# A two-layer attention and feed-forward network: expert tiles and layer 1's rotation put into one stage

## The chip, the cores and the metric

One core of one Trainium2 chip runs the kernel. The metric is the device time of one execution in microseconds (us). The core has TensorE (PE; its weight loads are PEld), VectorE (DVE), ScalarE (ACT), GpSimd (POOL), SyncE (SP, here only a queue of DMAs) and 16 DMA engines. Names such as `a_ov` or `q_ps` are on-chip tensors; TensorE writes to PSUM, which GpSimd doesn't reach.

## The reference

A sequence of 2048 tokens of 128 numbers goes through two layers. Each layer is `x + attention(xn) * silu(ffn(xn))`, with `xn` the layer norm of x. All is float32.

```python
# layer 1 (H = 16 heads of 64, E = 8 experts, F = 512)
q, k, v = split(xn @ qkv_w.T)                       # 16 heads each
q, k = rope(q), rope(k)      # t1*c - t2*s, t1*s + t2*c over the two halves of a head
attn = softmax(q @ k.T * 0.125 - p * log1p(a * |i - j|))
s = (attn @ v) @ out_w.T
probs = softmax(xn @ Wr + br); idx = argmax(probs)  # one expert a token
h = relu((layernorm(xn) * g + b) @ W1[idx] + b1[idx])
y = (h @ W2[idx] + b2[idx]) * max(probs)
x = x + s * silu(y)
```

Layer 0 has attention without rotation and bias, and a feed-forward with ternary weights and gelu.

## The kernel before

The program is a row of stages. Each is a block in which every engine has an instruction list written out by hand, ordered against the others by semaphores; a stage ends when all engines and its DMAs are through. For layer 1 they are:

`layernorm_stage` (L84), which leaves `xnT`, the transposed activations.

`route_stage` (L995). TensorE multiplies `xnT` by the router weights (L1057). A long chain of small VectorE steps takes the maximum, the one-hot choice and running counts; TensorE adds the counts over the partitions (`tot` and `pos`, L1061 to L1063); from these comes for each token its place in a list sorted by expert, padded to 23 tiles (`TL`) of 128 tokens of one expert each. Then VectorE normalizes and scales each of the 16 token tiles (L1126 to L1131) and GpSimd scatters it to the DRAM tensor `sorted_in` (L1050). SP loads all experts' weights meanwhile, the first matrices into `w1` and the second into a part of `va`.

`expert_tiles_stage` (L1151). TensorE spreads the biases, reads the owner of each of the 23 tiles from `tiles` into registers (`value_load`), and then works a tile at a time: transposes of four tiles at once (L1211), four upward products (L1222) with the weights that GpSimd has picked from `w1` (L1256), relus shared by ScalarE (L1277) and VectorE (L1295), a bias product (L1231) and four downward products (L1236). VectorE copies the results out (L1288), SP stores them to `sorted_out` (L1193). While tile i is up, tile i-1 goes down.

`qkv_stage(nc, k, 1, w1, rope=table)` (L367). First 16 value tiles: two 128x512 products each (L536), half copied by ScalarE (L490), half by VectorE (L447), to `va`. Meanwhile GpSimd gathers each token's result from `sorted_out` into `gate` (L512) and copies layer 1's output weights into `wo` (L515). Then 32 rotation jobs, one for each of 8 pairs of heads, q or k, and half of the sequence: TensorE makes the product with the weights and with a copy of them whose halves are exchanged and signed (`wsw`, L443, L550), 1024 columns of each; VectorE multiplies the first by the cosines and the second by the sines (L464, L465); GpSimd adds the two (L518); ScalarE rounds the sum to float16, the high part (L502); VectorE subtracts this from the sum, the low part (L455), two jobs late. SP stores both (L406, L407). `t1` and `t2` have three buffers, the float16 parts two. At the end ScalarE applies silu to `gate` (L506).

`attention_stage(nc, k, 1, bias=True)` (L565). SP loads q, k and a table of biases (L629 to L637). GpSimd clears tensors (L922 to L925). VectorE takes maxima over 16 pieces (L840), ScalarE turns them into a row (L772, L777), then for each of 512 steps: scores (L688), bias added by VectorE (L878), exponent by ScalarE (L784), values (L699), sums by GpSimd (L943).

Of the kernel before, what the change touches and what calls it, by code (L numbers as in the profile page):

```python
# [564 lines left out]
def attention_stage(nc, k, layer, bias=False):  # L565

    with ExitStack() as ctx:
# [25 lines left out]
        added = m.sem(g + "added") if bias else None  # L593
# [172 lines left out]
        def _(act):  # L766
# [152 lines left out]
        def _(pool):  # L919
# [62 lines left out]
def experts_stage(nc, k, t, fetched):  # L982

    with ExitStack() as outer:
# [3 lines left out]
        w1 = mo.sb("ex_w1", [D, NE, FF])  # L988
        scattered, weights_loaded = mo.sem("ex_scattered"), mo.sem("ex_weights_loaded")
        w2 = flat(k.va[:, :, :])[:, 0:FT * NE * D].rearrange("p (j e d) -> p j e d", j=FT, e=NE)  # L990
        route_stage(nc, k, t, tiles, hot, w1, w2, scattered, weights_loaded)
        expert_tiles_stage(nc, k, t, tiles, hot, w1, w2, scattered, weights_loaded, fetched)


def route_stage(nc, k, t, tiles, hot, w1, w2, scattered, weights_loaded):  # L995

    with ExitStack() as ctx:
# [19 lines left out]
        tot = m.ps("rt_tot", [P, NE])  # L1017
        loaded, affine_loaded, made, counted, chain = (m.sem("rt_loaded"), m.sem("rt_affine"), m.sem("rt_made"),
# [8 lines left out]
        def _(sp):  # L1027
# [4 lines left out]
            sp.dma_start(w1[:, :, :], t["L1_ffn_W1"].rearrange("e m f -> m e f")).then_inc(weights_loaded, 16)  # L1032
# [5 lines left out]
        def _(pool):  # L1038
# [7 lines left out]
            nc.gpsimd.memset(ends[:, :, 0:NE], 0.0).then_inc(counted, 1)  # L1046
            pool.wait_ge(placed, 1)
# [6 lines left out]
        def _(pe):  # L1054
            pe.wait_ge(loaded, 32)
            for q in range(NT):
                last = nc.tensor.matmul(ps[:, q, :], k.xnT[:, q * P:(q + 1) * P], wr[:, :], start=True, stop=True)  # L1057
            last.then_inc(made, 1)
            pe.wait_ge(counted, 6)
# [4 lines left out]
                             start=False, stop=True).then_inc(ranked, 1)  # L1064

# [78 lines left out]
        def _(act):  # L1144
            act.wait_ge(var_done, 1)
            nc.scalar.activation(std[:, :], std[:, :], ACT.Sqrt).then_inc(std_done, 1)
            act.wait_ge(shifted, 1)
            nc.scalar.activation(e[:, :, :], e[:, :, :], ACT.Exp).then_inc(exped, 1)


def expert_tiles_stage(nc, k, t, tiles, hot, w1, w2, scattered, weights_loaded, fetched):  # L1151

    with ExitStack() as ctx:
        m = Memory(nc, ctx)
        b1, b2 = m.sb("ep_b1", [NE, FF]), m.sb("ep_b2", [NE, D])
        b1t = m.sb("ep_b1t", [P, FT, TL])
        room = flat(k.va[:, :, :])[:, FT * NE * D:]
        xs = room[:, 0:TL * D].rearrange("p (i d) -> p i d", d=D)
        xsT = room[:, TL * D:2 * TL * D].rearrange("p (i q) -> p i q", q=P)
        ys = room[:, 2 * TL * D:3 * TL * D].rearrange("p (i d) -> p i d", d=D)  # L1160
        hT = room[:, 3 * TL * D:3 * TL * D + 2 * FF].rearrange("p (b j q) -> p b j q", b=2, j=FT)
        w1i = m.sb("ep_w1i", [P, 2, FF])
        tp = m.ps("ep_tp", [P, 2, 4, P])
        up = m.ps("ep_up", [P, 2, 2, 512])
        dn = m.ps("ep_dn", [P, 2, 4, D])
        bt = flat(dn[:, 1, :, :])[:, 0:FT * TL].rearrange("p (j i) -> p j i", j=FT)
        loaded, xs_loaded, turned, xs_copied = (m.sem("ep_loaded"), m.sem("ep_xs_loaded"), m.sem("ep_turned"),
                                                m.sem("ep_xs_copied"))
        spread, b1_copied, up_done = m.sem("ep_spread"), m.sem("ep_b1_copied"), m.sem("ep_up_done")
        w1_picked = m.sem("ep_w1_picked")  # L1170
        relu_act, relu_dve, dn_done, y_copied = (m.sem("ep_relu_act"), m.sem("ep_relu_dve"), m.sem("ep_dn_done"),
                                                 m.sem("ep_y_copied"))
        block = ctx.enter_context(nc.Block())
        NG = (TL + 3) // 4

        def members(g):
            return range(4 * g, min(4 * g + 4, TL))

        @block.sync
        def _(sp):  # L1180
            sp.dma_start(b1[:, :], t["L1_ffn_b1"]).then_inc(loaded, 16)
            sp.dma_start(b2[:, :], t["L1_ffn_b2"]).then_inc(loaded, 16)
            sp.wait_ge(scattered, 16 * NT)
            for g in range(NG):
                a, b = 4 * g, members(g)[-1] + 1
                sp.dma_start(xs[:, a:b, :], k.sorted_in[a * P:b * P, :].rearrange("(i p) d -> p i d", p=P))\
                  .then_inc(xs_loaded, 16)
                if g % 2 == 1 or g == NG - 1:
                    sp.wait_ge(xs_loaded, 16 * (g + 1))
            for g in range(NG):  # L1190
                a, b = 4 * g, members(g)[-1] + 1
                sp.wait_ge(y_copied, g + 1)
                sp.dma_start(k.sorted_out[a * P:b * P, :].rearrange("(i p) d -> p i d", p=P), ys[:, a:b, :])\  # L1193
                  .then_inc(fetched, 16)
            sp.wait_ge(fetched, 16 * NG)

        @block.tensor
        def _(pe):
            pe.wait_ge(loaded, 32)
            for j in range(FT):  # L1200
                last = nc.tensor.matmul(bt[:, j, :], b1[:, j * P:(j + 1) * P], hot[:, :], start=True, stop=True)
            last.then_inc(spread, 1)
            owners = [pe.value_load(tiles[0:1, i:i + 1], min_val=0, max_val=NE - 1) for i in range(TL)]

            def turn(g):
                if g % 2 == 0:
                    pe.wait_ge(xs_loaded, 16 * min(g + 2, NG))
                if g >= 2:
                    pe.wait_ge(xs_copied, g - 1)
                for i in members(g):  # L1210
                    last = nc.tensor.transpose(tp[:, g % 2, i % 4, :], xs[:, i, :], k.ident[:, :])  # L1211
                last.then_inc(turned, 1)

            def upward(i):
                if i % 4 == 0:
                    pe.wait_ge(xs_copied, i // 4 + 1)
                pe.wait_ge(w1_picked, i + 1)
                if i >= 2:
                    pe.wait_ge(relu_act, i - 1)
                    pe.wait_ge(relu_dve, i - 1)  # L1220
                for j in range(FT):
                    last = nc.tensor.matmul(up[:, i % 2, j // 2, (j % 2) * P:(j % 2 + 1) * P], w1i[:, i % 2, j * P:(j + 1) * P], xsT[:, i, :],  # L1222
# [3 lines left out]
            def downward(i):  # L1226
                g = i // 4
                o = dn[:, g % 2, i % 4, :]
                if i % 4 == 0 and g >= 2:
                    pe.wait_ge(y_copied, g - 1)  # L1230
                nc.tensor.matmul(o, hot[:, i:i + 1].broadcast_to([NE, P]), b2[:, :], start=True, stop=False)  # L1231
                pe.wait_ge(relu_act, i + 1)
                pe.wait_ge(relu_dve, i + 1)
# [5 lines left out]
            turn(0)  # L1239
            pe.wait_ge(weights_loaded, 16 * (1 + FT))  # L1240
            for i in range(TL):
                if i % 4 == 0 and i // 4 + 1 < NG:
                    turn(i // 4 + 1)
                upward(i)
                if i >= 1:
                    downward(i - 1)
            downward(TL - 1)

        @block.gpsimd
        def _(pool):  # L1250
            pool.wait_ge(weights_loaded, 16 * (1 + FT))
            for i in range(TL):
                owner = pool.value_load(tiles[0:1, i:i + 1], min_val=0, max_val=NE - 1)
                if i >= 2:
                    pool.wait_ge(up_done, i - 1)
                nc.gpsimd.tensor_copy(w1i[:, i % 2, :], w1[:, bass.ds(owner, 1), :].rearrange("p a f -> p (a f)"))                  .then_inc(w1_picked, 1)  # L1256

        @block.scalar
        def _(act):
            act.wait_ge(spread, 1)  # L1260
# [3 lines left out]
            def copy_x(g):  # L1264
                act.wait_ge(turned, g + 1)
                n = len(members(g))
                nc.scalar.activation(xsT[:, 4 * g:4 * g + n, :], tp[:, g % 2, 0:n, :], ACT.Copy).then_inc(xs_copied, 1)

            copy_x(0)
            for i in range(TL):  # L1270
                if i % 4 == 0 and i // 4 + 1 < NG:
                    copy_x(i // 4 + 1)
                act.wait_ge(up_done, i + 1)
                if i >= 2:
                    act.wait_ge(dn_done, i - 1)
                for j in range(2):
                    last = nc.scalar.activation(hT[:, i % 2, j, :], up[:, i % 2, 0, j * P:(j + 1) * P], ACT.Relu,  # L1277
                                                bias=b1t[:, j, i:i + 1])
                last.then_inc(relu_act, 1)

        @block.vector
        def _(ve):
            ve.wait_ge(b1_copied, 1)

            def copy_y(g):
                ve.wait_ge(dn_done, members(g)[-1] + 1)
                n = len(members(g))
# [91 lines left out]
```

## Time and profile before

| what | us |
|---|---|
| median of 3 runs | 3075.92 (3074.8 to 3075.96) |
| the profiled execution | 3079.59 |
| its span | 3077.9 |
| PE, DVE, ACT, POOL busy | 2807.8, 2504.0, 1557.4, 2502.6 |
| mean granted TensorE clock | 0.964 |

The span is the time from the first to the last instruction that the profiler recorded. Busy times of the engines overlap. A granted clock of 1.00 is TensorE's full 2.4 GHz, 0.50 is 1.2 GHz. Attention takes some 85% of the span (layer 0 to 1431 us, layer 1 from 1730 us); the stages that the change touches lie between.

### The profile page before, as it was taken

To read this page: it belongs to the slowest core of one execution; us is meant where nothing else is said; L and a number is where in the kernel's file an instruction comes from. 1 tells how busy PE (TensorE), PEld (TensorE's weight loads), DVE (VectorE), ACT (ScalarE), POOL (GpSimd) and SP (SyncE) were. 2 spreads that over 40 slices of the span, in tenths; PEclk is the share of its full clock that TensorE was granted. 3 is DMA by queue.
4 is the path that set the end of the run, shared out by engine and by line. 5 is a ranking of instruction groups with operands and counts; after the bars stand their busy time and mean duration, and the time that the engine had idled before them with its cause. 6 is when DMAs were issued, how large, how long until landed. Compare 5 with 4: busy or idle time off the path is not lost. (4 is left out here: it accounts for less than half of the span.)

```text
span 3077.9 us, 46733 instructions
## 1 busy us (share of the span) xinstructions
PE 2807.8 (91%) x17656; PEld 1147.6 (37%) x17656; DVE 2504.0 (81%) x3379; ACT 1557.4 (51%) x1889; POOL 2502.6 (81%) x1205
## 2 busy tenths in 40 slices
PE   5959999999999999996499599999999999999997
PEld 3413333333333333333354133333333333333332
DVE  6568888888888888874339699999999999999995
ACT  4325555555555555552122255555555555555554
POOL 0009999999999999994339389999999999999997
PEclk9979999999999999997699699999999999999998
DMA  4250111111111111101203501111111111111100
GB/s 109 86 191 22 35 29 28 28 28 28 28 28 28 28 29 28 28 1 38 60 27 137 190 4 52 55 55 55 55 55 55 55 55 55 55 55 55 55 1 14
DMA packets 63825, 155.28 MB, mean 50 GB/s; under 512 B 18017, under 2 KB 33770, under 8 KB 61426
## 3 DMA queue, kind: packets, MB, share of 16 engines
q1 hardware_dynamic: 62578, 150.20, 17.4%
q8 instruction: 141, 2.31, 0.3%
q0 software_dynamic: 1024, 2.10, 0.2%
q14 instruction: 82, 0.67, 0.1%
HBM read 113.34 MB, written 38.93 MB: 49 GB/s over the span
## 5 line engine op out<-in xcount | busy, mean ns | idle before, releaser
L943 POOL TENSOR_TENSOR a_sums<-a_sums,room 128x1024 f32<-128x1024 f32 x512 | 1195.4, 2364 | 83.1 <-ACT room L795 42.5
L699 PE MATMUL a_ov<-room,va 128*64 128x512 f32 x4096 | 994.0, 606 | 0.0
L784 ACT ACTIVATE room<-room,sscale 128x1024 f32<-128x1024 f32 x512 | 588.3, 1149 | 539.3 <-DVE room L878 539.2
L845 DVE TENSOR_REDUCE a_mx<-a_jb 128x1 f32<-128x1024 f32 x501 | 611.9, 1221 | 129.6 <-PE a_jb L653 123.4
L943 POOL TENSOR_TENSOR a_sums<-room 128x1024 f32<-128x1024 f32 x256 | 604.3, 2361 | 116.6 <-ACT room L784 66.8
L840 DVE CUSTOM_DVE_ANT_0 a_junk<-a_jb,a_tab 128x1024 bf16<-128x1024 f32 x501 | 610.5, 1219 | 83.2 <-PE a_jb L653 74.8
L878 DVE TENSOR_TENSOR room<-a_st,a_tab 128x1024 f32<-128x1024 f32 x512 | 622.9, 1217 | 12.4 <-PE a_st L688 10.2
L795 ACT ACTIVATE room<-a_st,sscale 128x1024 f32<-128x1024 f32 x256 | 285.3, 1114 | 360.1 <-PE a_st L688 360.1
L652 PE MATMUL a_jb<-a_kh,a_qh 64*128 64x512 f16 x1002 | 384.9, 384 | 66.1 <-DVE a_mx L840 32.1
L699 PEld LDWEIGHTS a_ov<-room,va 128*64 128x64 f32 x4096 | 248.7, 136 | 409.3 <-issue 372.7
L688 PE MATMUL a_st<-a_qh,a_kh 64*128 64x512 f16 x2048 | 395.6, 383 | 3.0 <-DVE a_mx L840 2.9
L688 PE MATMUL a_st<-a_ql,a_kh 64*128 64x512 f16 x2048 | 390.8, 378 | 0.0
L688 PE MATMUL a_st<-a_qh,a_kl 64*128 64x512 f16 x2048 | 390.6, 378 | 0.0
L865 DVE SCALAR_TENSOR_TENSOR room<-a_rows,a_st 128x1024 f32<-128x1024 f16 x256 | 312.7, 1221 | 92.3 <-PE a_st L688 90.9
L653 PE MATMUL a_jb<-a_kh,a_qh 64*128 64x512 f16 x1002 | 385.1, 384 | 0.0
L788 ACT ACTIVATE room<-room,sscale 128x1024 f32<-128x1024 f32 x256 | 294.0, 1148 | 170.8 <-DVE room L865 170.8
L946 POOL TENSOR_TENSOR a_sums<-a_sums 128x1024 f32<-128x1024 f32 x128 | 302.8, 2366 | 10.1
L688 PE MATMUL a_st<-a_rows,a_lower 64*128 64x512 f16 x1536 | 292.9, 378 | 0.0
L652 PEld LDWEIGHTS a_jb<-a_kh,a_qh 64*128 64x128 f16 x1002 | 93.6, 93 | 465.8 <-DVE a_mx L845 306.3
L688 PEld LDWEIGHTS a_st<-a_qh,a_kh 64*128 64x128 f16 x2048 | 99.8, 94 | 274.0 <-issue 164.1
L950 POOL TENSOR_TENSOR a_total<-a_sums 128x512 f32<-128x512 f32 x128 | 162.5, 1270 | 10.0
L710 PE MATMUL a_xb<-ones,a_total 128*128 128x1 f32 x1024 | 136.4, 254 | 17.3 <-POOL a_total L950 17.3
(219 smaller groups left out, 2642.6 us busy)
## 6 DMA issues: line engine op xcount, KB each, us to landing
a_tab<-bias_line SPq DMA_DIRECT2D x16, 1984.0 KB, 11.0
qk_high<-q_oh SPq DMA_DIRECT2D x32, 512.0 KB, 2.6
qk_low<-q_ol SPq DMA_DIRECT2D x32, 512.0 KB, 3.6
a_qh<-qk_high SPq DMA_DIRECT2D x64, 256.0 KB, 4.5
a_kh<-qk_high SPq DMA_DIRECT2D x64, 256.0 KB, 5.1
a_ql<-qk_low SPq DMA_DIRECT2D x64, 256.0 KB, 7.5
a_kl<-qk_low SPq DMA_DIRECT2D x64, 256.0 KB, 7.8
ex_w<-in_L_ffn_W SPq DMA_DIRECT2D x1, 2048.0 KB, 10.5
```

The lines of the kernel that those rows point to most:

```text
L652: nc.tensor.matmul(o[:, 0:QC], qh[0:DH, q0:q0 + P], kh[0:DH, k0:k0 + QC], start=True, stop=True)
L653: nc.tensor.matmul(o[:, QC:2 * QC], qh[DH:P, q0:q0 + P], kh[DH:P, k0 + QC:k0 + 2 * QC], start=True, stop=True).then_inc(max_ready, 1)
L688: last = nc.tensor.matmul(st[:, step % 2, t * QC:(t + 1) * QC], w, x, start=(r == 0), stop=(r == len(rounds) - 1))
L699: last = nc.tensor.matmul(ov[t * DH:(t + 1) * DH, :], k.va[:, 2 * s + t, h * DH:(h + 1) * DH], prob[:, step % RING, t * QC:(t + 1) * QC], ...
L784: nc.scalar.activation(prob[:, r, :], prob[:, r, :], ACT.Exp, scale=k.sscale[:, layer:layer + 1])\
L788: nc.scalar.activation(prob[:, r, :], prob[:, r, :], ACT.Exp, scale=k.sscale[:, 0:1])\
L840: nc.vector.tensor_tensor_reduce(out=junk[:, i % 2, :], in0=scratch(n, j), in1=tab[:, n // NC % 2, c0:c0 + 2 * QC][:, ::-1], scale=1.0, sc ...
L845: nc.vector.reduce_max(mx[:, j // 2, j % 2:j % 2 + 1], scratch(n, j), AX.X).then_inc(max_done, 1)
L865: nc.vector.scalar_tensor_tensor(p, high, -float(MAXROW), x, ALU.mult, ALU.add).then_inc(lowered, 1)
L878: nc.vector.tensor_tensor(p[:, :, ::-1], x[:, :, ::-1], window, ALU.add).then_inc(added, 1)
L943: nc.gpsimd.tensor_tensor(a, first, prob[:, step % RING, :], ALU.add).then_inc(summed, 1)
L946: nc.gpsimd.tensor_tensor(a, a, sums[:, (n + 1) % 2, :], ALU.add).then_inc(summed, 1)
```

## The change

Three stages (route, expert tiles, q/k/v of layer 1) become two.

In the route stage TensorE also makes the first 8 value tiles, three of them ahead of the rank products `tot` and `pos`, five behind; ScalarE copies them to `va`. GpSimd regroups the q and k weights into `wo`: for each group of four heads, the first halves of the heads side by side (128 columns), then the second halves. The second experts' and first experts' weights both go to the second half of `va`, so `ex_w1` is gone. The expert biases are loaded here.

`experts_and_rotation_stage` does the rest. It has 16 rotation jobs: 4 groups of four heads, q or k, half of the sequence. A job makes the product with the first halves (`low_part`) and with the second halves (`high_part`), one PSUM buffer of 1024 columns each. VectorE multiplies each by cosines and by sines (four multiplies), GpSimd subtracts two and adds two, ScalarE makes two high parts and VectorE two low parts, one job late. Into TensorE's and ScalarE's lists two expert tiles are put in each of jobs 1 to 11 and one in job 12, behind the job's own work (`project` on TensorE, `high_halves` of the job before on ScalarE); the last 8 value tiles go into jobs 12 to 15. ScalarE does all that other engines did for the tiles: the picks, all four relus, both copies. Transposes and downward results have one PSUM buffer instead of two. TensorE and ScalarE each read the 23 owners into registers.

The gathers and silus move into the attention stage: the gathers behind GpSimd's clears, the silus behind ScalarE's first row and ahead of its first exponent.

```diff
@@ attention_stage, ScalarE and GpSimd @@
             divide_maxima(0)
             row(0)
+            if bias:
+                act.wait_ge(gathered, 16 * NT)
+                for q in range(NT):
+                    nc.scalar.activation(k.gate[:, q, :], k.gate[:, q, :], ACT.Silu, scale=k.prob[:, q:q + 1])
...
             nc.gpsimd.memset(lower[DH:DH + 1, :], -float(MAXROW)).then_inc(ones_set, 1)
+            if bias:
+                for q in range(NT):
+                    nc.gpsimd.indirect_dma_start(k.gate[:, q, :], None, k.sorted_out[:, :],
+                                                 bass.IndirectOffsetOnAxis(ap=k.spot[:, q:q + 1], axis=0))\
+                      .then_inc(gathered, 16)
@@ route_stage, GpSimd, TensorE, ScalarE @@
+            for i in range(2):
+                for r in range(2):
+                    nc.gpsimd.tensor_copy(grouped[:, i, r, :, :], halves[:, i, :, r, :])
             pool.wait_ge(placed, 1)
...
             last.then_inc(made, 1)
+            def values_of(q):
+                if q >= 2:
+                    pe.wait_ge(val_copied, q - 1)
+                for c in range(2):
+                    last = nc.tensor.matmul(val[:, q % 2, c * QC:(c + 1) * QC], k.xnT[:, q * P:(q + 1) * P],
+                                            k.w1[:, 2, c * QC:(c + 1) * QC], start=True, stop=True)
+                last.then_inc(valued, 1)
+            for q in range(3):
+                values_of(q)
             pe.wait_ge(counted, 6)
             pe.wait_ge(added, 1)
...
+            for q in range(3, NVAL):
+                values_of(q)
...
+            for q in range(NVAL):
+                act.wait_ge(valued, q + 1)
+                nc.scalar.activation(k.va[:, q, :], val[:, q % 2, :], ACT.Copy).then_inc(val_copied, 1)
@@ experts_and_rotation_stage, TensorE @@
+            def project(j):
+                g, i, half = jobs[j]
+                for r, (part, ready) in enumerate(((low_part, a_ready), (high_part, b_ready))):
+                    if j >= 1:
+                        pe.wait_ge(prod, 4 * (j - 1) + 2 * r + 2)
+                    for c in range(2):
+                        q0 = half * 1024 + c * 512
+                        last = nc.tensor.matmul(part[:, c * 512:(c + 1) * 512], wqk[:, i, r, g * P:(g + 1) * P],
+                                                k.xnT[:, q0:q0 + 512], start=True, stop=True)
+                    last.then_inc(ready, 1)
...
+            project(0)
+            owners = [pe.value_load(tiles[0:1, i:i + 1], min_val=0, max_val=NE - 1) for i in range(TL)]
             pe.wait_ge(weights_loaded, 16 * (1 + FT))
+            for j in range(NJOB):
+                if j >= 1:
+                    project(j)
+                for i in work[j]:
...
+                    if i % 4 == 0 and i // 4 + 1 < NG:
+                        turn(i // 4 + 1)
+                    upward(i)
+                    if i >= 1:
+                        downward(i - 1)
...
+                for q in late[j]:
+                    values_of(q)
@@ ScalarE @@
+            for j in range(NJOB):
+                if j >= 1:
+                    high_halves(j - 1)
+                for i in work[j]:
+                    if i == 0:
+                        copy_x(0)
+                    if i % 4 == 0 and i // 4 + 1 < NG:
+                        copy_x(i // 4 + 1)
+                    act.wait_ge(up_done, i + 1)
+                    if i >= 2:
+                        act.wait_ge(dn_done, i - 1)
+                    for f in range(FT):
+                        last = nc.scalar.activation(hT[:, i % 2, f, :], up[:, i % 2, f, :], ACT.Relu,
+                                                    bias=b1t[:, f, i:i + 1])
+                    last.then_inc(relu_done, 1)
+                    if i + 2 < TL:
+                        pick(i + 2)
+                    if i % 4 == 0 and i >= 4:
+                        copy_y(i // 4 - 1)
...
@@ VectorE and GpSimd @@
+            def low_halves(j):
+                for r, rotated in enumerate((first, second)):
+                    ve.wait_ge(high, 2 * j + r + 1)
+                    nc.vector.tensor_tensor(split[:, j % 2, 1, r, :], rotated[:, j % 2, :], split[:, j % 2, 0, r, :],
+                                            ALU.subtract).then_inc(low, 1)
+            for j, (g, i, half) in enumerate(jobs):
+                b, sl = j % 2, slice(half * 1024, (half + 1) * 1024)
+                ve.wait_ge(a_ready, j + 1)
...
+                nc.vector.tensor_tensor(first[:, b, :], low_part[:, :], cos[:, sl], ALU.mult).then_inc(prod, 1)
+                nc.vector.tensor_tensor(second[:, b, :], low_part[:, :], sin[:, sl], ALU.mult).then_inc(prod, 1)
+                ve.wait_ge(b_ready, j + 1)
...
+                nc.vector.tensor_tensor(product[:, 0, :], high_part[:, :], sin[:, sl], ALU.mult).then_inc(prod, 1)
...
+                nc.vector.tensor_tensor(product[:, 1, :], high_part[:, :], cos[:, sl], ALU.mult).then_inc(prod, 1)
+                if j >= 1:
...
+                    low_halves(j - 1)
...
+                pool.wait_ge(prod, 4 * j + 3)
+                nc.gpsimd.tensor_tensor(first[:, b, :], first[:, b, :], product[:, 0, :], ALU.subtract).then_inc(rot, 1)
+                pool.wait_ge(prod, 4 * j + 4)
+                nc.gpsimd.tensor_tensor(second[:, b, :], second[:, b, :], product[:, 1, :], ALU.add).then_inc(rot, 1)
+            nc.gpsimd.tensor_copy(flat(k.wo[:, :, :]), flat(k.wo1[:, :, :]))
```

## Rows read from the trace of the kernel before

**Rows 1.** Windows by stage: length, busy time of each engine (instructions), granted clock, DMA, GB/s.
```profile
1449.00:1491.50 42.50, 8.62 (x38) 8.26 (x38) 26.21 (x114) 1.81 (x3) 16.93 (x22) 0.50 0.45 127
1491.50:1571.50 80.00, 62.38 (x445) 56.19 (x445) 18.04 (x52) 18.12 (x53) 14.17 (x23) 0.86 0.14 39
1571.50:1730.40 158.90, 143.06 (x320) 59.37 (x320) 126.22 (x114) 49.43 (x65) 120.38 (x49) 0.95 0.29 113
```

**Rows 2.** Groups, q/k/v stage: busy us, mean ns, idle before and its releaser.
```profile
L502 ACT ACTIVATE q_oh<-q_t 128x1024 f16<-128x1024 f32 x32 | 33.8, 1057 | 88.3 <-POOL q_t L518 88.3
L515 POOL COPY wo<-wo 128x2048 f32<-128x2048 f32 x1 | 1.9, 1907 | 0.0
```

**Rows 3.** Timeline, q/k/v stage: start us, us, instruction, idle before in brackets.
```profile
1577.49 0.60 ACT L490 ACTIVATE va<-q_ps 128x512 f32<-128x512 f32 x1 [1.12 <-PE q_ps L536]
...
1616.48 1.23 DVE L464 TENSOR_TENSOR q_t<-q_ps,rope 128x1024 f32<-128x1024 f32 x1
1617.62 1.22 DVE L465 TENSOR_TENSOR q_t<-q_ps,rope 128x1024 f32<-128x1024 f32 x1
1618.75 1.22 DVE L455 TENSOR_TENSOR q_ol<-q_t,q_oh 128x1024 f16<-128x1024 f32 x1
1620.07 1.23 DVE L464 TENSOR_TENSOR q_t<-q_ps,rope 128x1024 f32<-128x1024 f32 x1
```

**Rows 4.** Timeline of GpSimd, the rotation's first jobs.
```profile
1608.47 2.35 POOL L518 TENSOR_TENSOR q_t<-q_t 128x1024 f32<-128x1024 f32 x1 [13.42 <-DVE q_t L465]
...
1618.92 3.27 POOL L518 TENSOR_TENSOR q_t<-q_t 128x1024 f32<-128x1024 f32 x1 [0.32 <-DVE q_t L465]
```

**Rows 5.** Line L455 (min/median/max ns), then the timeline at the rotation's end.
```profile
L455 DVE TENSOR_TENSOR q_ol<-q_t,q_oh x32: 1215/1215/3361, 1615.2 to 1724.3; 128x1024 f16<-128x1024 f32 x32
...
1719.68 4.49 DVE L455 TENSOR_TENSOR q_ol<-q_t,q_oh 128x1024 f16<-128x1024 f32 x2
1719.84 3.25 POOL L518 TENSOR_TENSOR q_t<-q_t 128x1024 f32<-128x1024 f32 x1 [0.34 <-DVE q_t L465]
...
1724.34 1.23 DVE L455 TENSOR_TENSOR q_ol<-q_t,q_oh 128x1024 f16<-128x1024 f32 x1 [0.17 <-ACT q_oh L502]
```

**Rows 6.** Timeline of the expert tiles.
```profile
1515.49 1.06 PE L1222 MATMUL ep_up<-va,ep_w1i 128*128 128x128 f32 x8
...
1516.59 0.63 ACT L1277 ACTIVATE va<-ep_up,ep_b1t 128x128 f32<-128x128 f32 x2 [1.77 <-PE ep_up L1222]
...
1517.89 1.06 PE L1222 MATMUL ep_up<-va,ep_w1i 128*128 128x128 f32 x8
...
1520.92 0.60 ACT L1267 ACTIVATE va<-ep_tp 128x512 f32<-128x512 f32 x1 [1.31 <-PE ep_tp L1211]
```

**Rows 7.** Timeline of the tile stage's start; last a window, columns as in rows 1.
```profile
1493.35 1.90 PE L1201 MATMUL ep_dn<-ex_hot,ep_b 8*128 8x23 f32 x8 [28.52 <-DMA ep_b<-in_L_ffn_b]
1508.59 1.96 PE L1211 MATMUL ep_tp<-ident,va 128*128 128x128 f32 x8 [13.34 <-issue]
...
1514.00:1515.00 1.00, 1.00 (x8) 0.80 (x7) 0.61 (x2) 0.62 (x2) 0.62 (x1) 1.00 0.00 0
```

**Rows 8.** The route stage: the group of the scatters, then its timeline.
```profile
L1050 POOL DMA_INDIRECT sorted_in<-acc,spot x16 | 15.9, 992 | 23.4 <-DVE acc L1131 19.7 <-issue 3.6
...
1452.03 7.00 PE L1057 MATMUL rt_ps<-rt_w,room 128*128 128x8 f32 x32 [3.91 <-DMA rt_b<-in_L_ffn_br]
1463.21 0.56 PE L1061 MATMUL rt_tot<-rt_before,ones 128*128 128x8 f32 x2 [4.18 <-DVE rt_before L1107]
```

**Rows 9.** Timeline of the attention stage's start.
```profile
1733.30 0.20 POOL L925 MEMSET a_lower<- 1x128 f16 x1
...
1754.63 1.28 ACT L784 ACT_TABLE_LOAD   x1
...
1766.05 1.23 DVE L878 TENSOR_TENSOR room<-a_st,a_tab 128x1024 f32<-128x1024 f32 x1 [1.95 <-PE a_st L688]
```

More of the change, by code:

```diff
@@ L1169, in expert_tiles_stage @@
[L1169 to L1172, printed above, removed]
+        b1t = m.sb("er_b1t", [P, FT, TL])
+        first, second, product = (m.sb("er_first", [P, 2, 1024]), m.sb("er_second", [P, 2, 1024]),
+                                  m.sb("er_product", [P, 2, 1024]))
@@ L1173, in expert_tiles_stage, with xs @@
         block = ctx.enter_context(nc.Block())
         NG = (TL + 3) // 4
+        jobs = [(g, i, half) for g in range(4) for i in range(2) for half in range(2)]
+        NJOB = len(jobs)
+        work = [[i for i in range(TL) if 1 + i // 2 == j] for j in range(NJOB)]
+        late = [[q for q in range(NVAL, NT) if NJOB - (NT - q + 1) // 2 == j] for j in range(NJOB)]
         def members(g):
             return range(4 * g, min(4 * g + 4, TL))
+        def xs(a, b):
+            return k.acc[:, a:b, :] if b <= NT else xs_more[:, a - NT:b - NT, :]
@@ L1179, in _, with xsT @@
+        def xsT(a, b):
+            return xsT_first[:, a:b, :] if b <= NT else xsT_more[:, a - NT:b - NT, :]
         @block.sync
         def _(sp):
[L1181 to L1189, printed above, removed]
@@ new lines, in store_qk @@
+            def store_qk(j):
+                g, i, half = jobs[j]
+                sp.wait_ge(low, 2 * j + 2)
+                for n, store in enumerate((k.qk_high, k.qk_low)):
+                    rows = store[i].rearrange("a p s -> (a p) s").rearrange("(g h r d) s -> g r h d s", g=4, h=4, r=2)
+                    for r in range(2):
+                        sp.dma_start(rows[g, r, :, :, half * 1024:(half + 1) * 1024], split[:, j % 2, n, r, :])\
+                          .then_inc(stored[j % 2], 16)
@@ L1197, in _ @@
+            for b in range(2):
+                sp.wait_ge(stored[b], 64 * (NJOB // 2))
+            sp.wait_ge(y_stored, 16 * NG)
         @block.tensor
         def _(pe):
[L1199 to L1203, printed above, removed]
+            def project(j):
+                g, i, half = jobs[j]
+                for r, (part, ready) in enumerate(((low_part, a_ready), (high_part, b_ready))):
[6 more added lines that the diff above has]
+                    last.then_inc(ready, 1)
@@ L1237, in downward @@
                 last.then_inc(dn_done, 1)
-            turn(0)
-            pe.wait_ge(weights_loaded, 16 * (1 + FT))
[L1241 to L1256, printed above, removed]
+            pe.wait_ge(biases_loaded, 32)
@@ L1258, in _, with pick, copy_values @@
         @block.scalar
         def _(act):
+            owners = [act.value_load(tiles[0:1, i:i + 1], min_val=0, max_val=NE - 1) for i in range(TL)]
+            act.wait_ge(weights_loaded, 16 * (1 + FT))
+            def pick(i):
+                nc.scalar.activation(w1i[:, i % 2, :], w1[:, bass.ds(owners[i], 1), :].rearrange("p a f -> p (a f)"),
+                                     ACT.Copy).then_inc(picked, 1)
+            def copy_values(q):
+                for c in range(2):
+                    act.wait_ge(valued, 2 * (q - NVAL) + c + 1)
+                    nc.scalar.activation(k.va[:, q, c * QC:(c + 1) * QC], flat(up[:, c, :, :]), ACT.Copy)\
+                      .then_inc(val_copied, 1)
@@ L1266, in copy_x @@
                 n = len(members(g))
[L1267 to L1279, printed above, removed]
+                nc.scalar.activation(xsT(4 * g, 4 * g + n), tp[:, 0:n, :], ACT.Copy).then_inc(xs_copied, 1)
```

186 lines of the change are left out of this document (122 added, 64 removed).

## The prediction, made before the kernel was changed

> **What bounds the kernel now.** I read the windows by stage first [rows 1]. The change touches the 281 us from 1449.0 to 1730.4 (route, expert tiles, layer 1's q/k/v) and the first 36 us of the attention after it. In the route stage every engine is mostly idle; in the tiles TensorE is busy 62 of 80 us and VectorE 18; in the q/k/v stage VectorE is busy 126 of 159 us. So the expert tiles are TensorE's, the rotation is VectorE's, and one could lie beside the other.
>
> ScalarE's high half is 1.06 us [rows 2]. One value tile is two 128x512 float32 products, and while TensorE sets the pace a copy of 0.60 us comes after 1.12 us of waiting for it [rows 3]: 1.72 us a tile, so the four products of a rotation job are 3.43 us.
>
> The timeline of VectorE [rows 3] shows such a job: two multiplies that start 1.14 us apart, then the subtract that makes the low half, next job 1.32 us after it starts: 3.59 us a job, 115 us for 32. GpSimd's add [rows 4] took 2.35 us when no subtract was near and 3.27 us when it was issued at 1618.92, 0.17 us behind the subtract at 1618.75. Read as a lock: the subtract holds something for about 1.09 us, the add waits 0.92 us and then takes its 2.35. The end of the stage shows the other order [rows 5]: an add issued at 1719.84 waits for the subtract of 1719.68, ends at 1723.09 (again 0.9 + 2.35), and the next subtract, issued at about 1720.8, ends only at 1724.17: the two subtracts are 4.49 us instead of about 2.4. A multiply, which reads one operand from PSUM, shows no such thing: it is 1.22 us beside adds throughout [rows 3, 4].
>
> The Trainium skill says the same in "SBUF — State Buffer", section "Who interferes with whom": a VectorE instruction with two SBUF inputs and a GpSimd instruction that reads SBUF exclude each other for a whole instruction, and "issue order, not op shape, decides who blocks". The trace agrees in both orders (3.27 against 2.35 us for the add, 4.49 us for two subtracts).
>
> In the tile stage [rows 6] a tile is 2.40 us of TensorE (1515.49 to 1517.89), two relus are 0.63 us on ScalarE, a four-tile copy 0.60. At the stage's start [rows 7] TensorE ends its bias products at 1495.25 and does nothing that the profile names ("issue") until 1508.59: those are the 23 value_loads of the owners, 13.3 us, 0.58 each. It then works at 0.50 of the clock and is at 1.00 from 1514: 5.4 us at the lower level (1.2 GHz) after an idle stretch.
>
> **The change part by part.**
>
> Route stage. GpSimd's four regrouping copies fall into the 19.7 us in which it waits for the first scaled tile [rows 8]; the whole 128x2048 copy is 1.91 us [rows 2], so four quarters are 2 to 4 us: nothing. If they reached past that wait the stage would end later by the excess. The scatters then take 15.9 + 3.6 = 19.5 us and end the stage, so whatever delays VectorE's rank chain delays all. Here something does: three value tiles stand on TensorE between the router products (end 1459.0) and the rank products (start 1463.2) [rows 8]. They are 5.2 us at full clock (rank products start at 1464.2, which then run at twice the speed: +0.4) and 10.3 us at half (+6.2). I take 5.4 us at the lower level and the rest at the upper, as in rows 7: 7.9 us, +3.8, less 0.8 for faster rank products: **+3.0 us**. The other five value tiles and ScalarE's eight copies (about 1.1 each) lie under the scatters. The new stage thus starts at 1494.5 instead of 1491.5.
>
> Start of the new stage (times from its start). Bias products to 2.0 [rows 7]; project(0), cold, low part at 5.5, high part at 8.1; then the same 23 value_loads, which now stand between project(0) and project(1): 13.3 us, to 21.4. project(1) is cold again, its low part is there at 24.8: VectorE, done with job 0 at about 10.3, starts **job 1 at 24.9**. ScalarE has 23 value_loads of its own (no row; 0 to 1 us each from TensorE's 0.58; I take 0.58, done at 13.4, hidden by TensorE's; at 1 us job 1's tiles come about 1 us later).
>
> A job in the new stage is half as many (16) and twice as large: four products (3.43 us, as before), four multiplies, two subtracts, two adds, two high halves. The multiplications by the other half no longer need their own products, so TensorE's rotation work falls from 110 to 55 us; VectorE's count stays 96. In plain VectorE time a job would be 2 x 3.59 = 7.2 us. But the order has changed. With S the start of a job: multiplies at S, +1.14, +2.28, +3.42; the first add needs the third multiply and starts at +3.57; the subtracts of the job before are issued from +4.55, while the add is running. By rows 5 the first subtract gets through at +5.92, ends about +7.0; the second add, waiting by then, goes ahead of the second subtract (as at 1720.8) to +9.33; that subtract ends at +10.4; the next job starts at **+10.6**. Both adds back to back give the same end: 3.57 + 2 x 2.35 + 2 x 1.09 = 10.45. Before, the subtract was issued 0.17 us ahead of its add and VectorE never waited. Bounds: 7.2 (no exclusion on VectorE's side) and 10.9 (full 1.22 us for each subtract).
>
> Do the tiles fit beneath 10.6 us? TensorE has 3.43 + 2 x 2.40 = 8.2 us a job, and 8.7 in every second one (four transposes, 0.45). ScalarE does the high halves first, the second at +9.4 to +10.5, then relus (1.2), picks (0.6), copies (0.6 each); in every second job the downward product waits for relu, pick and the copy of y: about 3.3 us after the second high half, so to S+4.7 of the following job with its own 1.4 us. project's low part is then ready at +6.4, needed at +10.6. So the 23 tiles cost nothing beside VectorE, and the 80 us stage goes; without the exclusion that chain is what is late next (rivals). ScalarE sums to 2.1 + 2 x 1.8 + 1.2 = 6.9 us a job. The last eight value tiles (3.43 us a job in four jobs) and their copies fit too. The stores are as many bytes; four issues a job instead of two for each pair of halves.
>
> End: job 15 starts at 24.9 + 14 x 10.6 = 173.3. Its second add ends at +9.3, job 14's subtract at +10.4, the weights' copy (1.9 us, GpSimd) goes next to +12.3, the last two subtracts end at +14.5. Before, the last subtract ended at 1725.57 and the next stage began at 1730.4, 4.8 us later, for stores and the barrier [rows 1, 5]; two more issues make it about 5.9: **193.7 us** for the stage.
>
> Attention of layer 1. Sixteen gathers (1.22 us each, 19.5) follow the memsets that end 3.1 us into the stage [rows 9]: last issue at 22.6, landed about 25.5 (estimate). ScalarE is free at 24.2 (1754.63), then a table load of 1.28, 16 silus (no row; 0.3 each as a half of a two-relu group, rows 6) 4.8, another load: with the landing at 25.5 about 32.9. The first exponent needs VectorE's sum that ends at 1767.27, 36.9: hidden with 4 us to spare. If that cover fails, every us past it is paid. The gathers share the DMA engines with the table that opens the stage; a MB beside 3.4 MB costs 0 to 4 us, I take **+2**. The silus that left the old stage ended together with its last stores, so their going gives under 1 us, counted in the end above.
>
> **Sum.** Old: 1491.5 to 1730.4. New end: 1494.5 + 193.7 = 1688.2, that is 42.2 us earlier; less 2: 40.2. The profiled execution took 3079.6 (span 3077.9 and 1.7 around it), 3.7 above the median of the runs, 3075.9; the difference is subtracted from the median: **3036 us**.
>
> **Rivals.**
>
> A. VectorE gets its second subtract in ahead of the waiting add, or is not held at all: for it speaks that the median old subtract took 1.215 us [rows 5], most with an add behind it; against it that the longest, 3.361 us, is the one which met an add that was first. Then TensorE and ScalarE set the pace: with the second add ending near +10.2 beside the subtracts, the downward product of every second job waits for high half, copy, relu, pick and copy, a 10.0 us job, the others 8.2; with the late value jobs the stage is 170 us: **3012**. With the adds also at 2.35 us and jobs at 7.2, about 2995.
>
> B. TensorE drops to the lower clock in the 2 to 3 us that it waits in each job and is slow to return. Each warm-up of 5.4 us costs 2.7, so a job's 8.2 to 8.7 become 10.9 to 11.4; with up to 1.3 us of waiting for ScalarE 12.5: 14 x 1.9 = 27 us more, **3062**. For it: rows 7; against: a busier TensorE waits less and so stays up.
>
> "TensorE: Matmul & The Clock Gate", section "HAM oscillation — how this bites in real kernels" of the Trainium skill describes short bursts that each start at the low clock after a wait; rows 7 show one such start, no row here a repeated one.
>
> C. The other side: TensorE stays at 1.2 GHz through the tile jobs, so that it is the bound. A job is 16.4 us, 17.4 with transposes; 11.5 such jobs cost (16.9 - 10.6) x 11.5 = 72 us: **3108**, slower. It decides from a mean tile job of 10.6 + 40.2 / 11.5 = 14.1 us. Against it: the dense tile stage rose to 1.00 within 5.4 us.
>
> D. The change doesn't overlap what it says at the seams: ranks at +6.2, ScalarE's loads slow, gathers past the first exponent by 8 us: **3050**.
>
> **How the numbers follow.** Forecast 0.55, A 0.22, B 0.09, D 0.10, C 0.04. The range from 3008 to 3058 holds the forecast, most of A and D and some of B. A measurement of this kernel tells 0.2% (6 us) from no change: faster 0.94, same 0.02, slower 0.04 (C).
>
> **What would show it.** In the changed trace: adds and subtracts of the new stage with subtracts of 2.4 to 3.4 us, VectorE's jobs 10.6 us apart while TensorE and ScalarE wait; 13 us of "issue" on TensorE after project(0); rank products 3 us later; the first exponent still released by VectorE's sum. Jobs under 9.5 us say A; a granted clock under 0.9 in the tile jobs says B or C.

## The result, and the profile after

The changed kernel takes **3056.64 us** (median of 4 runs, 3054.31 to 3060.03) beside 3075.94 for the kernel before on the same chip: ratio 0.9937, interval 0.992 to 0.9954. It is 19.3 us faster; 40 were forecast. The profiled execution took 3054.31 us, span 3052.5.

Windows of the changed kernel, columns as in rows 1: the route stage, the new stage, and a stretch near its end.
```profile
1444.60:1488.70 44.10, 23.40 (x70) 14.06 (x70) 26.17 (x114) 9.77 (x11) 19.08 (x26) 0.69 0.45 123
1488.70:1703.30 214.60, 148.77 (x605) 92.40 (x605) 161.26 (x96) 83.50 (x176) 92.11 (x33) 0.83 0.27 93
1674.00:1700.00 26.00, 1.48 (x4) 0.38 (x2) 6.34 (x4) 3.20 (x4) 5.73 (x2) 0.61 0.26 102
```
Against [rows 1] the route stage is 1.6 us longer (42.5 before), and one stage of 214.6 us replaces 80.0 + 158.9 = 238.9: 24.3 gained where the forecast had 45.2. In the last of the three windows the compute engines do little, and the DMA engines move 102 GB/s at a share of 0.26, about what four busy engines of sixteen give (0.25). The DMA records of the trace say the same: in these 26 us four packets of 2 KB, 84 ns each, are under way at once for 21.2 us and five for 4.6. In the kernel before, between 1640 and 1680, no packet is under way for 23.1 us and sixteen or seventeen for 12.2. (The changed part began 4.4 us earlier in this profiled execution than in the one before; layer 0, which is unchanged, was that much shorter.)

The start of the new stage, timeline of TensorE, then of ScalarE (start us, us, instruction, idle before).
```profile
1494.20 2.42 PE L1279 MATMUL er_high_part<-room,wo 128*128 128x512 f32 x4
1504.36 3.75 PE L1279 MATMUL er_low_part<-room,wo 128*128 128x512 f32 x4 [7.74 <-issue]
...
1501.30 1.15 ACT L1356 ACTIVATE w<-va 128x512 f32 x2 [29.05 <-issue]
```
The 23 value_loads leave TensorE idle for 7.7 us, not the 13.3 of [rows 7]: they ran, it seems, on its sequencer while the products already queued still executed. ScalarE's end at 12.6 us into the stage.

The first undisturbed job: VectorE, then GpSimd.
```profile
1508.15 1.22 DVE L1426 TENSOR_TENSOR er_first<-er_low_part,rope 128x1024 f32<-128x1024 f32 x1 [9.09 <-PE er_low_part L1279]
1509.29 1.21 DVE L1427 TENSOR_TENSOR er_second<-er_low_part,rope 128x1024 f32<-128x1024 f32 x1
1510.42 1.21 DVE L1431 TENSOR_TENSOR er_product<-er_high_part,rope 128x1024 f32<-128x1024 f32 x1
1511.56 1.21 DVE L1434 TENSOR_TENSOR er_product<-er_high_part,rope 128x1024 f32<-128x1024 f32 x1
1512.69 2.47 DVE L1418 TENSOR_TENSOR er_split<-er_first,er_split 128x1024 f16<-128x1024 f32 x1
1515.08 3.37 DVE L1418 TENSOR_TENSOR er_split<-er_second,er_split 128x1024 f16<-128x1024 f32 x1
1518.55 1.23 DVE L1426 TENSOR_TENSOR er_first<-er_low_part,rope 128x1024 f32<-128x1024 f32 x1
...
1511.72 2.36 POOL L1447 TENSOR_TENSOR er_first<-er_first,er_product 128x1024 f32<-128x1024 f32 x1 [9.05 <-DVE er_product L1431]
1514.03 3.34 POOL L1449 TENSOR_TENSOR er_second<-er_second,er_product 128x1024 f32<-128x1024 f32 x1
```
This is the exclusion of [rows 3], [rows 4] and [rows 5], in the order that was worked out: the add at 1511.72 holds the first subtract (2.47 us instead of 1.22), the second add goes ahead of the second subtract (3.37). The next job starts 10.40 us after this one.

Then comes what was not forecast: the chain from a store to VectorE. Timeline of ScalarE, TensorE and VectorE.
```profile
1532.48 1.06 ACT L1386 ACTIVATE er_split<-er_first 128x1024 f16<-128x1024 f32 x1 [8.54 <-DMA qk_low<-er_split]
...
1537.06 0.79 PE L1308 MATMUL er_dn<-ex_b,ex_hot 8*128 8x128 f32 x2 [6.15 <-ACT acc L1379]
...
1539.65 3.58 PE L1279 MATMUL er_low_part<-room,wo 128*128 128x512 f32 x4
...
1543.27 1.22 DVE L1426 TENSOR_TENSOR er_first<-er_low_part,rope 128x1024 f32<-128x1024 f32 x1 [4.03 <-PE er_low_part L1279]
```
Read it downwards. ScalarE wants to write the high half of a job into the buffer of two jobs before, whose stores haven't landed, and waits 8.5 us. Its copy `acc` (the expert's y), queued behind, is late; TensorE's downward product waits 6.2 us for it; the next rotation product, behind that, comes 4.0 us too late for VectorE. The view of waits of the new stage (engine, line, releaser: us in total, times, longest), ScalarE's and then the DMA queue's own:
```profile
ACT er_split L1386 <- DMA qk_low<-er_split: 79.5, 14, 8.5
...
SPq L1268 <- DMA qk_low<-er_split: 11.3, 1, 11.3
```
The profile page's DMA issues (KB each, median us to landing):
```profile
sorted_out<-acc SPq DMA_DIRECT2D x4, 256.0 KB, 12.2
```
A y tile of 256 KB takes 12.2 us to land; the kernel before needed 2.3 for the same transfer. And the end of the stage, VectorE then the DMA queue:
```profile
1684.64 1.22 DVE L1418 TENSOR_TENSOR er_split<-er_second,er_split 128x1024 f16<-128x1024 f32 x1
...
1687.03 4.54 SPq L1251 DMA_DIRECT2D qk_low<-er_split  x2
1703.30 0.51 SPq L629 DMA_DIRECT2D a_qh<-qk_high  x1
```
From the last subtract's end (1685.86) to the next stage are 17.4 us; 5.9 were forecast.

The arithmetic of the stores fits this: 64 of 256 KB are 16.8 MB, at 102 GB/s 164 us; a job's four are 10.3 us of transfer in a job of 10.4 us, and the y tiles' 1.5 MB queue in between.

### The profile page after: what moved, and what is told of

The parts are those of the page before. It is cut to its first block and busy times, and to the rows that moved or that the text cites. A ratio compares the mean times of both kernels' runs of the same rounds, so it can differ in the third digit from the quotient of the medians.

```text
span 3052.5 us, 46385 instructions
## 1 busy us (share of the span) xinstructions
PE 2762.6 (91%) x17528; PEld 1130.9 (37%) x17528; DVE 2520.1 (83%) x3309; ACT 1586.8 (52%) x1972; POOL 2476.2 (81%) x1186
## 3 DMA queue, kind: packets, MB, share of 16 engines
q0 software_dynamic: 1024, 2.10, 0.2%
```

## The experiments

Theory N (narrow stores): a store of the new stage names its target rows as 4 heads x 32 dimensions x 1024 columns, and the transfer is spread over as many DMA engines as that slowest dimension, 4, lets it. This is a rule of the Trainium skill, "DMA: Bandwidth & Descriptors", section "Why a DMA increments its semaphore by 16 and not by 1": the engines used are the largest number up to 16 that divides the slowest dimension of both patterns, and for one kind of queue they are always the lowest-numbered ones. The four packets at a time agree with the number; which engines they were, no row here shows. Rivals: the order of the rows in memory, SyncE's issues, or VectorE's long job itself.

**The stores' slowest dimension 32 instead of 4.** The columns of a group are put in the order dimension, head; SBUF rows follow, the rotation's frequencies are loaded in the same order (one transfer instead of four, in an early stage), and the rows written in DRAM are the same.
```
-grouped = flat(k.wo[:, :, :]).rearrange("p (i r h d) -> p i r h d", i=2, r=2, h=H)
+grouped = flat(k.wo[:, :, :]).rearrange("p (i r g d h) -> p i r g h d", i=2, r=2, g=4, h=4)
-rows = ...rearrange("(g h r d) s -> g r h d s", g=4, h=4, r=2)
+rows = ...rearrange("(g h r d) s -> g r d h s", g=4, h=4, r=2)
```


> The changed kernel with one thing else: within a group of four heads the rows are ordered by dimension first and head second (weights' columns and the angle table's partitions to match), so that the slowest dimension of each q/k store is 32 long instead of 4. Same bytes, same instructions. Theory (the stores ran on a part of the DMA engines: 102 GB/s at a DMA share of 0.26, so ScalarE waits for free buffers and the stage's end waits for the last stores): DMA share in bursts well over 0.26, no ScalarE wait for qk_low in the jobs, all jobs 10.4 us apart, stage end about 14 + 15 us earlier: 3056 - 29 = 3027 us. Rival 1 (the store path is limited by the 2 KB rows or by HBM writes, not by how it is spread): same time, 3056, still about 100 GB/s. Rival 2 (the stalls are ScalarE's order: tiles and high halves in one list): stalls stay, only the tail gains, 3041.

Measured: **3025.91 us** (3024.57 to 3028.75; ratio to before 0.9836, 0.982 to 0.9853), 30.7 below the changed kernel. Its VectorE, two jobs in the middle, and the landing of its y tiles:
```profile
1523.26 1.23 DVE L1426 TENSOR_TENSOR er_first<-er_low_part,rope 128x1024 f32<-128x1024 f32 x1
...
1533.66 1.23 DVE L1426 TENSOR_TENSOR er_first<-er_low_part,rope 128x1024 f32<-128x1024 f32 x1
```
```profile
sorted_out<-acc SPq DMA_DIRECT2D x4, 256.0 KB, 2.9
```
Jobs are 10.40 us apart without a gap, y tiles land in 2.9 us, ScalarE waits for no store, and the stage takes 184.1 us instead of 214.6. Between 1640 and 1660 no packet is under way for 14.3 us and sixteen to eighteen for 4.7: the stores come in bursts over all the engines. With the stores mended the kernel is 10 us faster than the forecast.

**VectorE's order.** The subtracts of the job before are put between the multiplies, each ahead of the add that it would meet: low part times cosines, high part times sines, first subtract, low part times sines, high part times cosines, second subtract. The waits of TensorE and GpSimd follow. Stores stay narrow.
```
-low*cos, low*sin, high*sin, high*cos, subtract, subtract
+low*cos, high*sin, subtract, low*sin, high*cos, subtract
```


> The changed kernel with VectorE's order in a job changed: low x cos, high x sin, first subtract, low x sin, high x cos, second subtract; GpSimd's adds are released accordingly. Stores as in the changed kernel. Theory of the exclusion (a subtract that finds an add running waits for its end): subtracts 1.22 us again, adds 2.35 plus at most 1.1; but the stores' 1.05 MB a job at 102 GB/s take 10.3 us, so jobs stay near 10 us apart and ScalarE's waits for stores grow: 3040 to 3056. Rival (subtracts are slow for another reason, such as their float16 output or length): they stay at 2.4 to 3.4 us. Rival to the store theory (stores do not bind): jobs 7.2 to 9 us apart, 3020 or less.

Measured: 3052.21 us (3048.11 to 3056.81; ratio 0.9925, 0.9908 to 0.9941), 4.4 below the changed kernel, whose runs overlap with these (from 3054.31). Its waits:
```profile
ACT er_split L1386 <- DMA qk_low<-er_split: 72.8, 14, 7.0
```
VectorE is quicker where no store holds it (jobs 1 to 3 start 9.2 and 8.2 us apart) and then has to wait (15.2 us to job 4): the stores are the bound of the changed kernel's stage.

**Both edits together.** The diff is the two above.

> Both edits: wide stores and the new VectorE order. If both theories hold they add up: jobs are then set by TensorE and ScalarE, 8.2 and 9.6 us alternately in the tile jobs, about 7.3 in the last ones, stage end about 56 us earlier than in the changed kernel: 3001 us. If only the stores matter 3027; if only the order 3040 to 3056.

Measured: **2999.69 us** (ratio 0.9755, 0.9739 to 0.9772). Timeline of VectorE and, last, GpSimd:
```profile
1560.17 1.23 DVE L1425 TENSOR_TENSOR er_first<-er_low_part,rope 128x1024 f32<-128x1024 f32 x1 [0.75 <-PE er_low_part L1279]
...
1563.03 1.22 DVE L1417 TENSOR_TENSOR er_split<-er_first,er_split 128x1024 f16<-128x1024 f32 x1
...
1566.43 1.22 DVE L1417 TENSOR_TENSOR er_split<-er_second,er_split 128x1024 f16<-128x1024 f32 x1
1568.83 1.22 DVE L1425 TENSOR_TENSOR er_first<-er_low_part,rope 128x1024 f32<-128x1024 f32 x1 [1.19 <-PE er_low_part L1279]
...
1563.19 3.27 POOL L1449 TENSOR_TENSOR er_first<-er_first,er_product 128x1024 f32<-128x1024 f32 x1 [1.56 <-DVE er_product L1429]
```
A subtract issued 0.16 us ahead of its add takes 1.22 us and the add 3.27, the order of [rows 4]; it is the order of issue that decides who waits, as the Trainium skill has it ("SBUF — State Buffer", section "Who interferes with whom"), and the run agrees. Now TensorE sets the pace, busy for all of the 16.88 us from 1551.95 to 1568.83: jobs of 8.66 and 8.22 us in turn, the 8.7 and 8.2 us that the prediction gave as TensorE's work. The 9.6 us expected of every second job did not appear; 10.9 us from job 12 to job 13 did, so that the sum of 3001 was met in part by luck. The same edit is worth 26.2 us beside wide stores and 4.4 beside narrow ones.

**Value_loads behind project(1)**, on top of both.
```
 project(0)
+project(1)
 owners = [pe.value_load(...) for i in range(TL)]
...
-    if j >= 1: project(j)
+    if j >= 2: project(j)
```


> As with both edits, and TensorE's 23 value_loads of the owners come after the products of job 1 instead of before. VectorE's wait of 9 us ahead of job 1 goes, but the tiles start as late as before and job 2's products stand behind the first two tiles: 0 to 2 us faster than with both edits, 3000. Rival (the whole 9 us is gained, since VectorE sets the pace): 2992.

Measured: 3005.37 us (ratio 0.9775, 0.9758 to 0.9791), 5.7 slower: a miss. TensorE, then VectorE:
```profile
1499.06 1.88 PE L1279 MATMUL er_high_part<-room,wo 128*128 128x512 f32 x4
1512.86 1.09 PE L1289 MATMUL er_tp<-ident,acc 128*128 128x128 f32 x4 [11.92 <-issue]
...
1522.53 1.23 DVE L1426 TENSOR_TENSOR er_first<-er_low_part,rope 128x1024 f32<-128x1024 f32 x1 [15.80 <-PE er_low_part L1279]
```
Job 1 starts early and job 2 late. The instructions of project(1) wait until VectorE has emptied project(0)'s products, and TensorE's sequencer with them. So only the last products (1.9 us) are queued when the loads begin, and 11.9 us are idle instead of 7.7; transposes, tile products and project(2) come after them.

**Two heads a store, and one head a store**, both on the changed kernel with its rows where they were; the counts waited for follow.
```
-sp.dma_start(rows[g, r, :, :, ...], split[:, ...])
+for h in range(0, 4, W):   # W = 2, or W = 1
+    sp.dma_start(rows[g, r, h:h + W, :, ...], split[32 * h:32 * (h + W), ...])
```


> The changed kernel with each store of four heads cut into two stores of two heads (8 issues a job instead of 4, the same rows, bytes and addresses, the semaphore's counts doubled). Theory: a store runs on as many DMA engines as the slowest dimension of its pattern lets it, the heads. With two heads it is two engines, always the same two: 51 GB/s and a share of 0.13 where four heads gave 102 GB/s and 0.26. The 16.8 MB of the stage then take 329 us instead of 164, the ScalarE and VectorE wait for the stores in every second job, and the kernel takes 3057 + 145 to 165 us: 3200 to 3225, slower than before the change. Rival (what limits the stores is the bytes, the bank behind them or the issue of SyncE, 0.6 us each and 4.8 us a job of 10.4): no longer than 3057, within 5 us.

Measured: 3207.34 us (2 runs, 3207.13 and 3207.55; ratio 1.043, 1.0409 to 1.0451). Window near the end of the stage, then the waits of the stage:
```profile
1840.00:1850.00 10.00, 0.00 (x0) 0.00 (x0) 0.00 (x0) 0.00 (x0) 0.00 (x0) 0.50 0.13 51
```
```profile
ACT er_split L1387 <- DMA qk_low<-er_split: 210.3, 14, 19.1
```
Half the slowest dimension, half the rate, 150.7 us more. In that window two packets are under way at once for 9.0 of the 10 us.

> The changed kernel with each store cut into four, one head each, so that the slowest dimension is the 32 rows of a head: 16 issues a job, 9.7 us of SyncE a job of 10.4, nothing else changed. Theory (the engines of a store are set by its slowest dimension): the stores run on 16 engines, the share in a stretch of the stage alternates between bursts and nothing, no wait for qk_low of over 1 us on ScalarE; jobs 10.4 us apart as in the run with the dimensions in the other order (3025.9), and a tail longer by 12 issues of 0.6 us: 3033 (3028 to 3040). Rival 1 (it was the order of the rows in memory or in the weights that cost): 3057. Rival 2 (SyncE's issues become the bound, as the y stores and their waits come on top of 9.7 us): jobs over 10.4 us apart, 3040 to 3055, with the SyncE busy throughout.

Measured: 3033.58 us (3032.38 to 3034.22; ratio 0.9865, 0.9848 to 0.9881). Window in mid-stage, then VectorE and the DMA queue in it:
```profile
1600.00:1620.00 20.00, 17.83 (x88) 12.52 (x87) 19.79 (x13) 10.18 (x24) 10.50 (x5) 0.92 0.46 114
```
```profile
1613.94 1.22 DVE L1427 TENSOR_TENSOR er_first<-er_low_part,rope 128x1024 f32<-128x1024 f32 x1
...
1624.32 1.23 DVE L1427 TENSOR_TENSOR er_first<-er_low_part,rope 128x1024 f32<-128x1024 f32 x1
...
1613.86 3.60 SPq L1252 DMA_DIRECT2D qk_high<-er_split  x8
1617.50 3.72 SPq L1252 DMA_DIRECT2D qk_low<-er_split  x8
```
Four times the issues (7.3 us of SyncE a job, where 9.7 were expected) and the same row order, and the jobs are back at 10.38 to 10.40 us. So it is neither the order of the rows, nor the bytes, nor the issues, but the slowest dimension: 2, 4 and 32 (in two ways) give 3207, 3057 and 3026 to 3034. The expectation's "no wait of over 1 us on ScalarE" was wrong: it waits 58.1 us in 14 pieces, 5.9 at the longest, since the last of a job's stores is issued 7 us after the first; VectorE's job is long enough to cover it.

**The value_loads in the route stage**, on top of both mends: the owners are worked out after the fourth scaled tile, and TensorE and ScalarE load them behind their value tiles, under the scatters.
```
     if q == 3:             # VectorE, after the scaled tile 3
+        ...                # reached, owner, then tiles; tiled += 1
 for q in range(3, NVAL): values_of(q)     # TensorE; ScalarE likewise
+pe.wait_ge(tiled, 1)
+k.pe_owners = [pe.value_load(...) for i in range(TL)]
```

> On top of both mends (dimension ahead of head in the stores; the VectorE's products in the order low times cos, high times sin, low times sin, high times cos), which took 2999.7 us: the tiles' owners are worked out after the fourth scaled tile of the route stage instead of at its end, and TensorE and ScalarE load them into registers there, under the scatters. Theory: the loads are 12.7 to 13.3 us of TensorE where nothing is queued in front, 7.7 beside the queued products of project(0); with them gone VectorE's job 1 starts 7.5 to 9 us earlier after the stage's start, ScalarE has its registers at once: 2991 (2989 to 2994). The five operations that come earlier on VectorE (some 1.5 us) delay the first scatters by as much only if VectorE leads them. Rival (the stage's start is held by another thing, xs tiles' loads and their landing, or ScalarE's first copies): under 3 us of gain, 2997 to 3001.

Measured: **2992.75 us** (2990.8 to 2993.51; ratio 0.973, 0.9714 to 0.9747), 6.9 less than with both mends. Timeline of TensorE in the new stage:
```profile
1501.09 1.19 PE L1284 MATMUL er_low_part<-room,wo 128*128 128x512 f32 x1 [2.54 <-DVE er_second L1439]
```
Job 1's products wait 2.5 us for VectorE, and no longer for loads. Job 1 starts 14.0 us after the stage's first product instead of 19.1: 5.1 us earlier, not the 7.5 to 9 expected, since VectorE has to empty job 0's products first. The time was met, the gain at the start was over-sized.

**All value tiles behind the rank products**, on top of that.
```
-for q in range(3): values_of(q)           # ahead of the rank products
-for q in range(3, NVAL): values_of(q)     # behind them
+for q in range(NVAL): values_of(q)
```

> As the one before, and the rank products of the route stage no longer have three value tiles of layer 1 ahead of them on TensorE: all value tiles follow the ranks. Theory: the first scatter comes 1.7 us earlier (the distance from the stage's start to the first scatter was 19.87 before the change and 21.61 after), and the last scatter and the next stage with it, since the scatters are one chain: 1.7 us less than the kernel before it, 2989 to 2990. Rival (the chain from the ranks to the scatters on VectorE and ScalarE has slack, or the value tiles now end after the last scatter): within 0.5 us of it or slower by up to 3.

Measured: 2992.19 us (2990.47 to 2993.57; ratio 0.9729, 0.9713 to 0.9746): 0.6 less, which these runs cannot tell from nothing. Its first and last scatter on GpSimd, then ScalarE, then TensorE:
```profile
1465.93 1.21 POOL L1074 DMA_INDIRECT sorted_in<-acc,spot  x1 [14.92 <-DVE acc L1168]
...
1485.28 0.96 POOL L1074 DMA_INDIRECT sorted_in<-acc,spot  x1 [0.31 <-issue]
...
1476.99 1.02 ACT L1187 ACTIVATE va<-rt_val 128x1024 f32<-128x1024 f32 x1 [0.69 <-PE rt_val L1088]
1490.09 1.15 ACT L1359 ACTIVATE w<-va 128x512 f32 x2 [12.07 <-PEq L1012]
...
1490.01 1.86 PE L1320 MATMUL er_tp<-ex_hot,ex_b 8*128 8x23 f32 x8 [13.05 <-PEq L1012]
```
The scatters do come earlier: the last one starts 29.1 us after VectorE's first operation on the router's result (1456.17), in the run before 31.0. The next stage gains little of it: it begins 3.8 us after the last scatter's end instead of 2.3. ScalarE ends its last value copy at 1478.0 and then does nothing named for 12.07 us, about what its 23 loads took in the changed kernel (12.6 us from the stage's start). TensorE is idle for 13.05 us behind its last value tile, about the 13.3 of its loads in [rows 7]. By these rows the loads of one engine or the other have become the last to end; which, they don't tell, and no run of its own tested it.

## Why the prediction missed

- **The step that failed**: "The stores are as many bytes; four issues a job instead of two for each pair of halves." The stores were costed at nothing by their bytes and priced only by their issues in the tail (5.9). Bytes fix a transfer's time only at a known rate, and the rate had changed: before, 128 rows of a pair of heads; now 4 heads x 32 rows, four packets at a time instead of sixteen. Jobs 1 to 15 started over 14.0 us more than 14 times 10.40, the last subtracts ended 3.7 us later after job 15's start than forecast, and the tail is 11.5 longer: 29 us in the trace. The runs agree: 30.7 us with the rows re-ordered, 23.1 with four times the issues.
- **VectorE's job**: forecast 10.6, measured 10.40. The exclusion, its order and its size were right; forecast subtracts "of 2.4 to 3.4", seen 2.47 and 3.37. Rival A is out: VectorE was held on both subtracts.
- **Job 1**: forecast 24.9 after the stage's start, measured 19.5. The value_loads were taken with the 13.3 of [rows 7], where only the bias products stood ahead; here 7.7. This is 5.4 us in the other direction.
- **Route**: rank products were forecast to end 3.0 us later and ended 1.7 later (17.5 us after the stage's start, 15.8 before); the first scatter with them (21.6 against 19.9). The three value tiles take 6.9 us, not 7.9.
- **Attention's start**: +2 forecast. The first sum of VectorE starts 35.84 us after the stage, before 35.5: +0.4. The silus took 4.78 as forecast, and are hidden with 3.7 us to spare:
```profile
1730.59 4.78 ACT L819 ACTIVATE gate<-gate,prob 128x128 f32<-128x128 f32 x16 [1.58 <-DMA gate<-sorted_out,spot]
1740.40 1.15 ACT L784 ACTIVATE room<-room,sscale 128x1024 f32<-128x1024 f32 x1 [3.74 <-DVE room L882]
```
- **The sum**: stage 193.7 forecast; less 5.4 (job 1), less 2.8 (14 jobs of 0.2), plus 14.0, 3.7 and 11.5 (stores) makes 214.7, and 214.6 was measured. With route (-1.4) and attention (-1.6) on their side too, the changed part came to 22.3 us less instead of 40.2 in the two profiled executions; the medians differ by 19.3.
- **The range**: 3056.64 lies inside 3008 to 3058, at its upper end, which was kept for D and some of B. That is luck: the stores stood in none of the cases the range was made from.
- **Rivals B to D** did not set the time. B and C have their sign (a granted clock of 0.83 over the stage, and again from 1600 to 1620), but in the tile jobs most of it follows from the stores: with wide stores alone the clock was 0.93 from 1600 to 1620, and jobs stayed 10.40 us apart; with both edits it was 0.95 from 1500 to 1600, and TensorE kept its 8.2 to 8.7 us a job. How much of the 14.0 us comes from TensorE at 1.2 GHz after a wait for stores was not separated. None of the four named the DMA engines.

## What to carry to other kernels

When a change alters how a transfer's rows are named, ask over how many DMA engines the new pattern is spread, not only how many bytes it moves: look at the slowest dimension on both sides, and in the profile for a DMA share that is flat at a fraction (0.26, 0.13) while something waits. Take a term's price from a row where the same work is queued in front. And where two engines exclude each other, the order of issue is free to choose: putting the short instruction just ahead of the long one was worth 26 us here, once nothing else was the bound.

## What the runs showed of the hardware

- Stores with slowest dimension 4 moved 102 GB/s at a share of 0.26, four packets at a time; with 2, 51 GB/s at 0.13, two at a time; with 32, sixteen to eighteen at a time in bursts. A 256 KB transfer of another kind among those with 4 took 12.2 us to land instead of 2.3 to 2.9.
- 23 value_loads left TensorE idle for 7.7 us behind the four products of project(0) (6.0 us of work), for 11.9 behind the last two of project(1) (1.9 us), and for 13.3 behind the bias products [rows 7]. These were 1.9 us of work too; why they covered less is not shown. On ScalarE the loads took 12.6 us at most.
- A store's issue on SyncE had a median of 0.43 us with one head (32 rows), 0.60 with 32 x 4 rows, and took 0.32 to 0.43 in the kernel before (128 rows named as one dimension). With two heads, where the stores pile up, the median was 2.4 us.
- A multiply (one operand from PSUM) was not held by an add: 64 of them in the changed kernel took 1.211 to 1.225 us, 64 in the run with both mends 1.215 to 1.226.
